# Norm refinement and the constant row on GpSimd, row sums moved, slots stored in one run

## The reference, cut to what matters

```python
x_norm = x / (norm(x, axis=-1) + 1e-08)          # x: Q or K of one head, 16 values
Qp, Kp = relu(x_norm @ projection) + 0.1          # 64 features per head
out = (Qp @ (Kp.T @ V)) / (Qp @ Kp.sum())         # per head
...
logits = xf @ router_w.T                          # top 2 of 8 experts per token
buf = zeros(E, capacity, H).at[flat_e, slot].add(dispatched)
h = silu(buf @ w1); out_buf = h @ w2              # then gathered back, weighted, summed
```

## Time and profile before

| | us |
|---|---|
| median of 3 runs (lowest to highest) | 1353.02 (1351.83 to 1355.73) |
| the profiled execution, its time | 1353.69 |
| its span | 1352.1 |

### The profile page before, as it was taken

One profiled execution on the slowest core, in us unless ns is written; L12 is line 12 of the kernel. 1 busy time (PEld: TensorE's weight loads), 2 busy tenths in 40 slices (PEclk: granted clock), 3 DMA queues, 4 the chain that ended last, 5 costly groups with the idle time before them and its releaser, 6 DMA issues.

```text
span 1352.1 us, 38635 instructions
## 1 busy us (share of the span) xinstructions
PE 1201.2 (89%) x14708; PEld 972.5 (72%) x14708; DVE 870.9 (64%) x2024; ACT 621.4 (46%) x1101; POOL 679.7 (50%) x646
## 2 busy tenths in 40 slices
PE   3779787878787888379999999999999999999997
PEld 1446464646564556259999999999999999989986
DVE  6778989898988886845555555554444444444442
ACT  3476767676757676333333333332222233233322
POOL 3313363636463637735555555555555555555542
PEclk9889798979888989589999999999999999999999
DMA  4111212112121111034444444433232332233330
GB/s 139 55 39 38 75 42 71 62 52 66 49 64 33 34 33 34 2 98 91 107 100 95 95 95 96 82 50 52 49 52 46 49 48 48 48 50 50 46 44 7
DMA packets 71788, 80.64 MB, mean 60 GB/s; under 512 B 14817, under 2 KB 65250, under 8 KB 71618
## 3 DMA queue, kind: packets, MB, share of 16 engines
q0 software_dynamic: 32288, 34.78, 17.1%
q1 hardware_dynamic: 39330, 43.39, 9.5%
HBM read 44.13 MB, written 34.92 MB: 58 GB/s over the span
## 4 chain that ended last, share of the span: by engine, by line
PE 66%; DVE 20%; issue 5%; ACT 4%; POOL 3%; DMA 1%; DVEq 0%; SPq 0%; ACTq 0%; POOLq 0%
PE bank L962 27%; PE bank L979 26%; DVE area L1369 4%; PE bank L703 2%; PE bank L823 2%; PE bank L946 2%; DVE area L1229 1%; PE bank L792 1%; DVE area L1378 1%; ACT area L502 1%; PE bank L809 1%; PE bank L764 1%; DVE area L1271 1%; DVE area L1360 1%; DVE area L1300 1%
## 5 line engine op out<-in xcount | busy, mean ns | idle before, releaser
L962 PE MATMUL bank<-area 128*128 128x256 f16 (+1 forms) x3408 | 376.7, 269 | 5.7 <-issue 3.1
L979 PE MATMUL bank<-area 128*128 x3240 | 365.3, 273 | 0.0
L962 PEld LDWEIGHTS bank<-area 128*128 x3408 | 324.7, 98 | 48.0 <-issue 7.8
L1549 DVE TENSOR_SCALAR area<-area 128x512 f16<-128x512 f32 (+1 forms) x284 | 125.3, 441 | 353.9 <-ACT area L629 350.7
L1173 POOL DMA_INDIRECT out_dram<-area,mt x135 | 218.4, 1618 | 247.4 <-ACT area L639 207.8
L979 PEld LDWEIGHTS bank<-area 128*128 128x128 f16 x3240 | 313.7, 98 | 35.6
L629 ACT ACTIVATE area<-bank 128x512 f32<-128x512 f32 (+1 forms) x284 | 163.7, 577 | 185.7 <-PE bank L962 184.2
L1078 POOL DMA_INDIRECT slot_table<-area x128 | 136.5, 1067 | 153.9 <-PE bank L823 96.7
L639 ACT ACTIVATE area<-bank,mt 128x256 f32<-128x256 f32 x135 | 57.1, 471 | 317.5 <-PE bank L979 317.5
L1551 DVE SCALAR_TENSOR_TENSOR area<-area 128x512 f16<-128x512 f32 (+1 forms) x284 | 189.5, 667 | 9.8
L1166 POOL DMA_INDIRECT xg<-xn_split,mt x135 | 135.4, 1003 | 42.6 <-issue 40.2
(11 more groups left out here) (195 smaller groups left out, 1485.4 us busy)
## 6 DMA issues: line engine op xcount, KB each, us to landing
w_raw<-in_w_dram SPq DMA_DIRECT2D x18, 512.0 KB, 4.4
area<-in_x_dram SPq DMA_DIRECT2D x16, 512.0 KB, 5.9
xn_split<-area SPq DMA_DIRECT2D x16, 512.0 KB, 2.9
out_dram<-area SPq DMA_DIRECT2D x32, 256.0 KB, 3.5
area<-in_w_dram SPq DMA_DIRECT2D x14, 512.0 KB, 4.6
xg<-xn_split,mt POOLq DMA_INDIRECT x135, 3.4
out_dram<-area,mt POOLq DMA_INDIRECT x135, 3.9
slot_table<-area POOLq DMA_INDIRECT x128, 2.8
```

The costliest lines, as they stand in the source:

```text
L962: mm = nc.tensor.matmul(big[j][:, i2 * n:(i2 + 1) * n], we[:, bass.ds(e * EXPERT + (k * 2048 + wl * 1024 + c * P), P)], moe_xT[t % XT][:, ...
L979: mm = nc.tensor.matmul(yb[:, a * D:(a + 1) * D], hT[u % 2][:, c, hl, a * P:(a + 1) * P], we[:, bass.ds(e * EXPERT + off, D)], start=(c == ...
L1549: v.tensor_scalar(hi, h, H_SCALE, None, ALU.mult).then_inc(mh_step, 1)
```

## The change

- `norm_refine` now refines both halves on GpSimd; VectorE only makes the guess, with scratch and input tiles of their own for each half. The refinement of half 0 stands behind the tenth scatter in GpSimd's queue.
- `constant_part` goes from VectorE to GpSimd, behind each of the two `x_low`; a new semaphore `const_ready` is waited for by the first drain of each half.
- `row_sums` of batch b+2 moves from behind `v_over_norm` 0 to behind `o_low` 1.
- The scatters run as 10 and 6 with one wait between the runs.
- ScalarE's `xn_high` of both halves go one place later.
- In the tail, both `constant_part` stand ahead of the 16 scatters of batch 7.

```diff
@@ act_turn
             k_relu(act, b, 3)
-            if body:
-                xn_high(act, b + 1, 0)
             act.wait_ge(gate_in, b + 1)
...
             if body:
+                xn_high(act, b + 1, 0)
+            q_relu(act, b, 0, 4, PAIRS)
+            if body:
                 xn_high(act, b + 1, 1)
-            q_relu(act, b, 0, 4, PAIRS)
@@ norm_refine
-            hold(pool, norm_guess, b + 1)
+            hold(pool, norm_guess, b * 2 + half + 1)
             for _ in range(3):
-                link(g.tensor_tensor(nu, nsq, ny, ALU.mult))
+                link(g.tensor_tensor(nu, nsq[half], ny[half], ALU.mult))
...
+        def constant_part(pool, b, half):
+
+            wait_read(pool, "attn", "cn", b)
+            if b > 0:
+                pool.wait_ge(o_split, b * 2 - 1 + half)
+            for t in range(HT):
+                ins = nc.gpsimd.tensor_tensor(nd[half][:, t], norm[:, half, t, 0:2, :].rearrange("p g e -> p (g e)").unsqueeze(2)
+                                              .broadcast_to([P, H, HD + 1]), cn_b, ALU.mult)
+            ins.then_inc(const_ready, 1)
@@ pool_turn
             if phase == "tail":
+                for half in range(2):
+                    constant_part(pool, b, half)
                 scatter(pool, b, 0, TOPK * NT)
                 return
             for half in range(2):
                 x_low(pool, b + 1, half)
+                constant_part(pool, b, half)
             if b > 0:
                 pool.wait_ge(attn_filled, nth("attn", f"ab{NT - 2}", b))
-                scatter(pool, b - 1, 0, 5)
-                pool.wait_ge(qk_filled, (b + 1) * QK_USES + 4)
-                scatter(pool, b - 1, 5, 10)
-                pool.wait_ge(qk_filled, (b + 1) * QK_USES + 8)
+                scatter(pool, b - 1, 0, 10)
+            norm_refine(pool, b + 1, 0)
+            if b > 0:
+                pool.wait_ge(qk_filled, (b + 1) * QK_USES + 6)
                 scatter(pool, b - 1, 10, TOPK * NT)
             if b == B - 2:
                 scatter(pool, b, 0, 3)
@@ start, on GpSimd
+            norm_refine(pool, 0, 0)
             norm_refine(pool, 0, 1)
@@ norms
-            if half == 1:
-                rsqrt_guess(chp, ny, nsq, nu, ready=norm_guess)
-                return
-            rsqrt_guess(chp, ny, nsq, nu)
-            for step in range(3):
...
-            chp.link(v.tensor_scalar(norm[:, 0], ny, 1e-8 * W_SCALE, None, ALU.add))
+            rsqrt_guess(chp, ny[half], nsq[half], nv, ready=norm_guess)
@@ v_over_norm
-            if half == 1:
-                dve.wait_ge(norm_ready, b + 1)
+            dve.wait_ge(norm_ready, b * 2 + half + 1)
@@ attend_drain
+            if t % HT == 0:
+                dve.wait_ge(const_ready, b * 2 + t // HT + 1)
@@ dve_turn
-            constant_part(dve, b, 0)
...
-            constant_part(dve, b, 1)
...
             o_low(dve, b, 1)
             if body:
+                if b + 2 < B:
+                    row_sums(dve, b + 2)
                 qk_halves(dve, b + 1, 1, 0, 4)
             out_drain(dve, phase, b, 0, first)
             if body:
                 v_over_norm(dve, b + 1, 0, chp)
-                if b + 2 < B:
-                    row_sums(dve, b + 2)
                 norms(dve, phase, b + 1, 1)
```

More of the change, by code:

```diff
@@ L241, in moe_attention @@
         nT = view([HS], F32)
-        nsq = view([HT, 4, 8], F32)
-        ny = view([HT, 4, 8], F32)
+        nsq = [view([HT, 4, 8], F32) for _ in range(2)]
+        ny = [view([HT, 4, 8], F32) for _ in range(2)]
         nu = view([HT, 4, 8], F32)
+        nv = view([HT, 4, 8], F32)
         norm = view([2, HT, 4, 8], F32)
@@ L338, in moe_attention @@
         kv_split = sem("kv_split")
+        const_ready = sem("const_ready")
         masks_ready = sem("masks_ready")
@@ L1052, in norm_refine @@
             g = nc.gpsimd
-            steps = [b * 13]
+            steps = [(b * 2 + half) * 13]
             def link(ins, apart=False):
@@ L1061, in link @@
                     pool.wait_ge(pool_norm, steps[0])
[L1063 removed]
+            hold(pool, norm_guess, b * 2 + half + 1)
             for _ in range(3):
[L1065 to L1066 removed]
+                link(g.tensor_tensor(nu, nsq[half], ny[half], ALU.mult))
+                link(g.tensor_tensor(nu, nu, ny[half], ALU.mult), apart=True)
                 link(g.tensor_scalar(nu, nu, -0.5, 1.5, ALU.mult, ALU.add))
[L1068 to L1069 removed]
+                link(g.tensor_tensor(ny[half], ny[half], nu, ALU.mult))
+            link(g.tensor_tensor(nu, nsq[half], ny[half], ALU.mult), apart=True)
             g.tensor_scalar(norm[:, half], nu, 1e-8 * W_SCALE, None, ALU.add).then_inc(norm_ready, 1)
+        def constant_part(pool, b, half):
[6 more added lines that the diff above has]
+            ins.then_inc(const_ready, 1)
         def scatter(pool, b, n0, n1):
@@ L1276, in norms @@
             src = drain(dve, phase, "prep", f"nrmT{half}", b)[:, :].rearrange("p (t g c) -> p t g c", t=HT, g=4)
-            v.tensor_copy(nsq, src[:, :, :, 0:8]).then_inc(prep_read, 1)
+            v.tensor_copy(nsq[half], src[:, :, :, 0:8]).then_inc(prep_read, 1)
             wait_read(dve, "prep", f"nrmT{half}", b)
-            if half == 1:
-                rsqrt_guess(chp, ny, nsq, nu, ready=norm_guess)
-                return
-            rsqrt_guess(chp, ny, nsq, nu)
-            for step in range(3):
[L1284 to L1288, removed]
-            chp.link(v.tensor_scalar(norm[:, 0], ny, 1e-8 * W_SCALE, None, ALU.add))
+            rsqrt_guess(chp, ny[half], nsq[half], nv, ready=norm_guess)
         def v_over_norm(dve, b, half, ch):
```

## The result

The changed kernel takes 1361.95 us (median of 5, 1360.60 to 1363.31), the kernel before 1353.02 in the same group (5 runs): a ratio of 1.0063, 95% interval 1.0050 to 1.0076. It is 8.9 us slower; 1365 was forecast, in a range from 1351 to 1375. The profiled execution took 1363.31 us, 9.6 more than the profiled one of before.

The account below looks back on a forecast made before the run. Turns were taken as bound by when the second refinement ends, behind one long GpSimd queue. Start, turns and tail summed to +12.2 us on the profiled 1353.7, 1365.9, predicted as 1365 against the median; range 1351 to 1375.

Parts of the forecast that it names:

- From the first scatter to the second norm: GpSimd's queue in a turn: sixteen scatters and both refinements, 35.75 us undisturbed, taken as 36.15; 34.8 before in turn 3.
- Turns 1 to 3: Change of turn length: +0.5 us each in turns 1 and 3, +1.5 in turn 2, earlier first scatter taken off.
- turn 6: Turn with 19 scatters, three more at 1.27 us each in GpSimd's queue: +4.4 us.
- turn 5: Second norm late by 2.15 us, taken as half hidden as in turn 4: +1.1 us.
- turn 4: Norm late by 1.5 us, but TensorE's last sums and an earlier drain decide: -1.0 us, bounds -2 and +1.5.
- turn 0: Turn without scatters, so the earlier guess of half 1 counts in full: -1.5 us.
- rival in which VectorE is the bound all through: Time taken off VectorE comes back at its reciprocal: 1306 us if all, 1346 at the small gain; chance 0.15.
- rival of the slow product: GpSimd's product takes 1.60 us, so the first drain waits in each turn: 1386 us; chance 0.05.
- Start: Before turn 0, refining half 0 takes 7.15 us on GpSimd instead of 3.2 on VectorE: +3.5 us.
- Tail: Eight products ahead of GpSimd's last 16 scatters: +4.5 us, less 1.35 of slack before the experts' first copy, net +3.2.
- Disturbance: Refinement of half 0 on GpSimd stretched beside VectorE's two-input `o_low` 1: 0.4 us a turn, bounds 0 and 1.2.
- gain at the front of a turn: First scatter earlier through constant rows (0.2 us) and ScalarE's order (0.65): 0.85 in turns 1 to 4, 0.2 in others.

Follow-up runs that it names:

- run that takes R0 out of it: The changed kernel with the refinement of half 0 on VectorE again, start included: 1356.54 us, ratio 1.0021 to the kernel before.
- run that delays the guess of half 1: The changed kernel with the row sums put back behind `v_over_norm` 0: 1366.35 us, ratio 1.0090 to the kernel before.
- run without the hold: The changed kernel without GpSimd's wait for the seventh attended tile ahead of a turn's first ten scatters: 1356.82 us, ratio 1.0023 to the kernel before.
- first group's chip: Chip of the follow-up runs that undid single parts of the change; the kernel before took 1354.23 us there (23 runs).
- second and third group: Later follow-up runs, each group on one other chip; the kernel before took 1398.87 us (29 runs) and 1394.35 us (17 runs) there.

## Why the prediction came out

**What was right.** The direction, and its mechanism. From the first scatter to the second norm, 35.75 us and 0.4 of disturbance were forecast; turn 3 shows 330.77 - 294.18 = 36.6. R1 starts behind the sixteenth scatter with no idle time, and half 0 hardly waits (0.8). The run that opens that queue sooner returns 5.2 us in the turns 1 to 6, the run that takes R0 out of it 8.2, of which 7.0 in turn 6; the run that delays the guess of half 1 leaves these turns as they are. Turns 1 to 3 together were forecast at +2.5 and measured +2.1, turn 6 +4.4 and +3.6, turn 5 +1.1 and +1.7, turn 4 -1.0 and -0.4, turn 0 -1.5 and -0.8. The rival in which VectorE is the bound all through is refuted by the 56.9 us that it waits, the rival of the slow product by 0.65 us.

The turns, read from the K-V copy that opens each (us; forecast in the last column where one number was used):

| turn | 1 | 2 | 3 | 4 | 5 | 6 | forecast |
|---|---|---|---|---|---|---|---|
| first scatter sooner by | 1.59 | 1.59 | 0.97 | 1.92 | 0.68 | 1.62 | 0.85 (1 to 4), 0.2 (5, 6) |
| first scatter to second norm, before | 34.75 | 33.76 | 34.78 | 33.78 | 34.15 | 35.62 | |
| the same, after | 36.57 | 36.41 | 36.58 | 37.19 | 36.54 | 40.37 | 36.15, turn 6 40.15 |
| second norm later by | 0.23 | 1.06 | 0.83 | 1.49 | 1.71 | 3.13 | |
| turn longer by | 0.22 | 1.06 | 0.82 | -0.38 | 1.71 | 3.62 | |

In turns 1, 2, 3 and 5 the turn grows by just what the second norm is late. That nothing of it is hidden in turn 5 goes against the forecast, which took 2.15 and half of it hidden; its +1.1 against +1.7 is near partly by luck.

**Terms that were mis-sized.**
- *Start*, +3.5 against +1.86. The step itself held (4.03 lost from guess to reciprocal; undoing it alone brings 2.5 us at the first copy). What came on top was a higher granted clock ahead of it in this execution, 1.86 us, which no row of before could tell. One of the runs shows the start without it: with the row sums put back, the eight sums take 1.91 us, the guess starts at 37.91, the first K-V sums at 63.67, 3.55 later than before and close to the 63.6 forecast, and the first copy at 73.76, 2.5 later. The other eleven runs and the changed kernel all have the sums at 1.07; of the kernel before there is only one trace, so how often it meets the lower clock isn't known.
- *Tail*, +3.2 against +1.54. The eight products with their hand-overs were put at 6.2; they took 4.87 in all, and lengthened the queue by 4.75. The idle 1.73 fell to the usual 0.30, as forecast. That makes +3.3 instead of +4.5. And the queue of the last 29 scatters opened 0.5 us sooner, counted from the turn's K-V copy. So from that copy to the last scatter's end it is 40.95 us against 38.2 before, +2.7, less 1.2 of slack. (The row at 553.28 in the earlier trace rows is the second scatter of batch 7, not the first, which starts at 550.59; the sum doesn't change by it.)
- *Disturbance*, 0.4 placed on R0. The queue is 0.7 to 1.4 us longer than the undisturbed 35.75 in turns 1 to 5. In turn 3 R0 was undisturbed (7.06 us); the scatters ahead of it paid. Ten of them took 14.5 us instead of 13.3: with the ten refinement steps gone, `o_low` 1 starts at 306.61 instead of 308.50 and falls on the tenth scatter, 1.76 us long; so it is in turns 2, 4 and 6 (1.60 to 1.98). In turns 1 and 5 it falls on R0, which takes 7.8 us. In the run without the hold it falls on R0 too, whose third step takes 1.36 instead of 0.30.

The Trainium skill (SBUF — State Buffer, Who interferes with whom) says that a VectorE instruction with two SBUF inputs contends with a GpSimd one that reads SBUF, and that the port pair they share is an exclusive lock. The arithmetic here agrees: 1.36 for 0.30, and VectorE's product 2.03 for 0.43 beside `x_low`. Of the issue of an indirect DMA the page infers that it would not contend with such an instruction; the rows differ (1.76 for 0.96), and the measurement decides.

**The step that failed** is the gain at the front of a turn: 0.85 in turns 1 to 4 and 0.2 in 5 and 6 were forecast, 0.7 to 1.9 came, 1.4 in the mean. What gave it can be followed in the two timelines of turn 3. The cast that builds the K-V matrix took 1.96 us and takes 0.30. Before, the second `x_low` ran beside it (274.78 to 276.90); now it starts at 283.06, and the first has ended 0.2 us ahead of the cast. That is ScalarE's order at work, since the run with the products back on VectorE has the cast at 0.30 too. It is 1.66 us gained, in turns 1 to 3 alike, where at most 0.7 was allowed for the order. The first drain then waits 2.30 us, more than the 1.5 allowed, for products that start only at 280.64, when ScalarE has copied `cn_b`. But that wait costs nothing, as VectorE next needs the relu of the fourth attended tile: `q_low` of half 1 starts 11.73 us after the turn's K-V copy (285.57) instead of 13.35, 1.6 sooner. In turns 1, 2 and 4 this gain reaches the scatters whole. In turn 3 it doesn't, because TensorE's granted clock falls from 1.00 (2.4 GHz) to 0.50 (1.2 GHz) between the two last groups of its feature matmuls. The first group had run at full clock; the second takes 1.46 us instead of 0.82, ScalarE and VectorE wait for it, and 0.97 is left. Two rows of the changed kernel, and the second group in the kernel before:

```profile
287.01 0.82 PE L811 MATMUL bank<-area,p_hl 32*128 32x512 f16 x6 [0.69 <-DVE area L1374]
288.20 1.46 PE L811 MATMUL bank<-area,p_hl 32*128 32x512 f16 x6 [0.37 <-DVE area L1374]
```

```profile
287.47 0.82 PE L809 MATMUL bank<-area,p_hl 32*128 32x512 f16 x6 [0.37 <-DVE area L1369]
```

So a front gain taken too small and a disturbance of the queue taken too small met near the right sum. That the two errors had opposite signs is luck.

**What stays open.** The loss of 0.6% was measured where the kernel before takes 1353 us, about what it takes on the first group's chip (1354). On the two slower chips the ratios are 1.0009 and 1.0016, and their intervals hold a loss of up to 0.4 and 0.5% as well as none. The kernel before was not profiled there, so it can't be said what it loses on such a chip that the changed one doesn't. The traces of the changed kernel there show VectorE waiting 1.6 to 4.8 us for half 1 instead of 5.9 and more, so the queue itself weighs less on these chips.

## What to carry to other kernels

Work taken off the busiest engine is worth little or nothing if the receiving engine has its queue between that work and the result on which the turn waits: add up that queue from the event that opens it to the result, and compare it with the arrival of the last input. An in-order queue gives back only down to its next input, so an edit that opens it earlier has to be priced against every release behind it, not the first. And a scatter's place is a choice of what it lies beside: look for two-input VectorE instructions, and for long runs of short matmuls.

## What the runs showed of the hardware

- Beside GpSimd's indirect DMAs (0.96 us each, one every 1.27), TensorE on the chips of the second and third group received a long run of short matmuls only one to five at a time, with up to 1.2 us between: 96 matmuls in some 15 us instead of 2.8. The first 50 of them passed at the usual pace. In the changed kernel on those chips the K-V sums of turn 6 come in this way beside the thirteen scatters of batch 6, on the second group's chip from 550.6 to 567.4 us, on the third's from 554.9 to 558.4, and that turn takes 89.85 and 82.65 us instead of 68.39. The cause of it (instructions that arrive late, or something else that holds TensorE's sequencer) is not shown; the profile says only "issue". The Trainium skill (Runtime: NRT & Kernel Launch, Instruction fetch mechanics) calls the fetching of instructions mostly hidden as long as the code doesn't branch; if that is what is starved here, these runs show a case in which it isn't.
- GpSimd's product of 128x272 with a broadcast input takes 0.636 to 0.658 us, 0.647 in the mean of 64, 1.5 times VectorE's 0.433. In a row they overlap: eight took 4.87 us, 0.61 each, where VectorE's take 0.37 each (23.8 us for 64).
- Beside these products in the tail, VectorE's own smallest instructions were stretched, a 128x16 product from 0.17 to 0.57, and a 128x16 TENSOR_SCALAR two instructions later from 0.24 to 0.58. The product in the changed kernel and before it:

```profile
558.74 0.57 DVE L1511 TENSOR_TENSOR area<-area 128x16 f32<-128x16 f32 x1
```

```profile
550.21 0.17 DVE L1517 TENSOR_TENSOR area<-area 128x16 f32<-128x16 f32 x1
```
